# A graph, attention and expert block on one core: expert weights merged by TensorE in groups of 32 columns, with four reorderings

## The chip, the core and the metric

One NeuronCore of a Trainium2 chip runs the whole program. The engines are TensorE (PE, with its weight loads as PEld), VectorE (DVE), ScalarE (ACT), GpSimd (POOL) and SyncE (SP), which issues the DMA transfers. The metric is the device time in microseconds.

## The reference

Input x has 1250 rows of 512 numbers, and 41,250 directed edges (src, dst). All is float32. Cut to what matters:

```python
# graph branch: linear + PReLU, then two layers of
agg = segment_sum(x[src], dst); h = prelu((x + agg) @ W1.T + b1) @ W2.T + b2
x = relu(batch_norm(h))
# mix branch (8 heads of 64): softmax(q) per row, softmax(k) over the rows
context = einsum('bnhd,bnhe->bhde', softmax_k, v / N); out = (q / 8) . context
mix = layer_norm(out @ w_out + b_out) * ln_scale
# expert layer on x2
gh = relu(x2 @ gfc1.T + b); g = (gh @ gfc2.T + b).mean(rows)      # 8 numbers
W1m = W1 + sum_e g[e] * tv_W1[e]; W2m = W2 + sum_e g[e] * tv_W2[e]  # 8 experts
b1m, b2m likewise; h = relu(x2 @ W1m.T + b1m); out = h @ W2m.T + b2m
result = (a layer norm of x2 + out) with merged scale and shift, added to the block's input
```

The expert weights of one kind are 8 matrices of 512 x 256 numbers, 8.4 MB for both kinds, and g is the same for all rows.

## The kernel before

The 1250 rows are 10 tiles of 125 (T), or 5 chunks of 250 columns when transposed (J). The 512 features are 4 blocks of 128 (KB). Every product is done in float16 with a high and a low part: 3 matmuls per block of the contraction, so 12 for a tile of 125 x 512 ("natural tile", `natural_tile`, L543 to L560) or for a block of 128 x 250 (`product`); all of them are issued by the line L462 of `passes`. ScalarE writes the high half of a result, VectorE the low half. GpSimd writes the low halves of the weights (`split_weight`, L1753).

Each engine has its own program, written out by hand in order; semaphores connect them. PSUM has 8 banks, given out in families: USES lists the phases of a family in order, RING its number of banks, and BANKS_FROM names what of another family must be read before a phase may take its banks. `wait_bank` turns this into waits.

Stages that the change touches:

**Query and value products (QV), from 120 us.** TensorE does the first 7 query tiles, then value and query tiles by turns, then value tiles alone. After each value tile comes a window: VectorE makes one-hot matrices of 15 edge columns (L1173 to L1185), its offsets (L1180) go to TensorE, which loads 15 addresses, multiplies the one-hots into a count bank (L448, L451), and ScalarE copies the counts to the adjacency matrix (L808). For each query tile VectorE takes maxima (L1359), subtracts (L1360), sums the exponentials (L1364), and GpSimd multiplies the tile by the reciprocal sums (L1771), in one loop over the ten tiles, when the sums are there.

**Mix, from 190 us.** The contexts times w_out give the m products in banks 0 to 3 (family z). Query tiles are flipped (`flip_q`, 4 transposes, L543) into two x banks; the loop over t flips tile t+4, then multiplies mix tile t into bank t % 2 (family n), then does a window. VectorE's loop does the window, the low part of tile t+4 (`low_tile_t`), then reads the mix tile (L1414). The first aggregation (agg0, L650) follows, in banks 0 to 3; it also needs the diagonal that VectorE adds (L1401).

**Expert layer, from 397 us.** Two 4 MB transfers bring tv, the expert weights (L420, L421), once the last down product is done. After the gate products (to 440.9 us) one small float32 matmul sums g. ScalarE makes 4 diagonal matrices g[e] * identity (L1106). TensorE multiplies expert matrices with them (`merge_on_pe`, L745), 128 x 512 results in float32, for 4, 3, 4 and 3 of the 8 experts of the four parts (two column halves of W1, two halves of W2: PE_SHARE); VectorE adds the other experts one at a time with scalar_tensor_tensor in halves of 256 (L1622) and then the bank of TensorE (L1629). ScalarE makes the high half of each part (L1110, L1116), VectorE the low half (L1195). TensorE's order: merge W1 part 0, the b2 matmul (L760), merge W1 part 1, ffn1 products 0 to 4, merge W2 parts 0 and 1, ffn1 products 5 to 9, then the ten last products (ffn2, `natural`, a bias matmul L772 and 6 more each) in two banks. `hidden(i)` on ScalarE and `low_hidden(i)` on GpSimd (L1814) turn an ffn1 product into the transposed hidden layer; the b2 row is split on GpSimd after `low_hidden(1)`.

**The tail.** The last tiles are handled in units of one or two tiles (UNITS). For a unit u VectorE adds the residual with row sums (L1682), scales the sums (L1686, row_minus), does `finish_unit(u - 1)` (reciprocal L1699, the add to the output for tiles that aren't GpSimd's, L1704) and `centre(u)` (L1692). ScalarE squares (L1138), takes the root (L1143) and then scales GpSimd's tiles of the unit before (`scale_unit`, L1132); GpSimd adds x for the tiles 1, 3, 5 and 7 (L1835). SyncE stores the tiles in order (L425), two transfers a tile.

Of the kernel before, what the change touches and what calls it, by code (L numbers as in the profile page):

```python
# [20 lines left out]
F32 = mybir.dt.float32  # L21
# [8 lines left out]
P = 125  # L30
# [46 lines left out]
PE_EXPERTS = 4  # L77
PE_SHARE = (4, 3, 4, 3)
# [8 lines left out]
for _t in range(T):  # L87
# [17 lines left out]
BANKS_FROM = {"qv": ("t", "k", 17), "mix": ("z", "m", 1), "agg0": ("n", "mix", 9), "ffn2": ("t", "ffn1", 9),  # L105
              "up1": ("x", "qt", T - 1), "rows": ("u", "up1", T - 1), "gnn": ("u", "up1", T - 3)}
# [18 lines left out]
UNITS = [(0, 1), (2, 3), (4, 5), (6, 7), (8,), (9,)]  # L125
# [28 lines left out]
def gps_block(nc, dram):  # L154

    with ExitStack() as ctx:
# [33 lines left out]
        def tr16(r, blocks=KB):  # L190
# [34 lines left out]
        g_diag = ohs[:, 2 * KB * CH + 6 * D:2 * KB * CH + 6 * D + PE_EXPERTS * 256].bitcast(F32).rearrange(  # L225
            "p (e n) -> p e n", e=PE_EXPERTS)
# [119 lines left out]
        def wait_bank(pe, family, phase, i, slot):  # L346
# [9 lines left out]
            if phase in BANKS_FROM:  # L356
                source, last, uses = BANKS_FROM[phase]
                if slot < min(RING[family], RING[source]):
                    wait_done(pe, source, last, uses + slot)
# [26 lines left out]
        def _(sp):  # L386
# [43 lines left out]
        def _(pe):  # L430
# [198 lines left out]
            for t in range(T):  # L629
                if t + 4 < T:  # L630
                    flip_q(t + 4)
# [109 lines left out]
            def merge_on_pe(bank_, part, share):  # L741

                for k in range(PE_EXPERTS - share, PE_EXPERTS):
                    pe.wait_ge(diag_ready, k + 1)
                    last = nc.tensor.matmul(bank_, g_diag[:, k, :], part(E - PE_EXPERTS + k), start=(k == PE_EXPERTS - share),  # L745
                                            stop=(k == PE_EXPERTS - 1))
                last.then_inc(pe_merged, 1)

            def merge_w1(bank_, m):
                merge_on_pe(ps[:, bank_, :].rearrange("p (k f) -> p k f", k=KB),  # L750
                            lambda e: tv[:, 0, e, :].rearrange("p (k f) -> p k f", k=KB)[:, :, m * 128:(m + 1) * 128], PE_SHARE[m])

            def merge_w2(bank_, h):
                merge_on_pe(ps[:, bank_, :], lambda e: tv[:, 1, e, h * D:(h + 1) * D], PE_SHARE[FB + h])

            pe.wait_ge(got_tv, 32)
# [1136 lines left out]
```

## Time and profile before

| | |
|---|---|
| median of 3 runs | 502.27 us (501.51 to 503.23) |
| the profiled execution | 499.22 us, its span 497.4 us |
| PE busy | 459.6 us, 92% |
| PEld / DVE / ACT / POOL busy | 357.8 / 324.2 / 250.1 / 168.9 us |
| chain of waits | PE 76%, DVE 13%, ACT 5%, issue 3%, POOL 2% |
| mean granted clock of TensorE | 0.989 |

The span is what the profiler saw from the first to the last instruction; the execution's own time holds 1.8 us around it. "Busy" of PE includes time in which a matmul waits in the pipe. The chain of waits is followed back from the last instruction, each step to what released it; "issue" is time for which the profile shows no cause. L with a number is a line of the kernel; where a helper issues everything, the tile names tell instructions apart.

### The profile page before, as it was taken

Reading aid. Unit: us, or ns where it says so; the run is one execution under the profiler, and the core shown is the slowest. Engines: PE = TensorE matmul, PEld = TensorE weight load, DVE = VectorE, ACT = ScalarE, POOL = GpSimd, SP = SyncE. Lnnn points to the kernel's source line nnn. Section 1 sums busy time; section 2 is a strip of 40 time slices with the busy share of each in tenths; the row PEclk is TensorE's granted clock in tenths of the full one; section 3 lists DMA queues with packets and bytes.
Section 4 is the critical chain, followed back from the end, with each engine's and each line's share of the span. In section 5 each row is a group of like instructions: output and inputs, shape, how many; then the busy total and the mean of one; then the engine's idle time right before and its main releaser. Section 6 shows DMA issues by size and latency. Waiting matters only on the chain.

```text
span 497.4 us, 9899 instructions
## 1 busy us (share of the span) xinstructions
PE 459.6 (92%) x3564; PEld 357.8 (72%) x3564; DVE 324.2 (65%) x749; ACT 250.1 (50%) x527; POOL 168.9 (34%) x176
## 2 busy tenths in 40 slices
PE   2999999999999998999999999999999969989892
PEld 1777668886765676766999995679998858956651
DVE  4777797747999857754655449635333676439787
ACT  4789345147712345244434756424446378734454
POOL 1379453021095003033336990004232124405412
PEclk9999999999999899999999999999999989999998
DMA  8702002202020002011100001000000296000024
GB/s 247 214 3 84 1 0 87 86 1 84 2 86 0 2 3 86 0 40 57 78 0 0 1 2 62 1 0 1 0 3 4 84 402 275 1 0 2 1 60 146
DMA packets 5246, 27.44 MB, mean 55 GB/s; under 512 B 1036, under 2 KB 1161, under 8 KB 3544
## 3 DMA queue, kind: packets, MB, share of 16 engines
q1 hardware_dynamic: 5208, 26.92, 15.6%
q8 instruction: 25, 0.41, 0.4%
q14 instruction: 13, 0.11, 0.1%
HBM read 24.36 MB, written 2.56 MB: 54 GB/s over the span
## 4 chain that ended last, share of the span: by engine, by line
PE 76%; DVE 13%; ACT 5%; issue 3%; POOL 2%; DMA 1%; SPq 0%; DVEq 0%; ACTq 0%
PE ps L462 47%; PE ps L650 17%; PE ps L451 4%; PE ps L745 3%; POOL late L1745 2%; PE ps L543 2%; PE ps L553 1%; DVE r L1692 1%; DVE late L1195 1%; DVE r L1704 1%; PE ps L448 1%; ACT r L825 1%; DVE ohs L1185 1%; DVE r L1682 1%; DVE offsets L1180 1%
## 5 line engine op out<-in xcount | busy, mean ns | idle before, releaser
L462 PE MATMUL ps<-r,wslot 128*128 128x250 f16 x840 | 95.3, 272 | 3.5 <-DVE r L1194 3.3
L462 PEld LDWEIGHTS ps<-r,wslot 128*128 128x128 f16 x840 | 81.5, 98 | 14.9 <-DVE r L1194 5.2
L650 PE MATMUL ps<-late,r 125*128 (+1 forms) x800 | 87.1, 269 | 1.0 <-DVE r L1414 1.0
L650 PEld LDWEIGHTS ps<-late,r 125*128 125x128 f16 x800 | 77.5, 97 | 10.9 <-issue 1.7
L1753 POOL TENSOR_TENSOR wslot<-stage,wslot 128x512 f16<-128x512 f32 x32 | 39.5, 1265 | 133.3 <-ACT wslot L797 133.3
L462 PE MATMUL ps<-wslot,r 128*125 128x512 f16 x300 | 70.5, 386 | 0.0
L462 PEld LDWEIGHTS ps<-wslot,r 128*125 128x125 f16 (+1 forms) x300 | 40.9, 139 | 22.1 <-issue 1.4
L1781 POOL TENSOR_TENSOR late<-ohs,late 128x250 f16<-128x250 f32 x40 | 25.7, 652 | 86.9 <-ACT late L980 86.9
L462 PE MATMUL ps<-late,wslot 128*128 (+1 forms) x480 | 51.7, 269 | 0.0
L462 PEld LDWEIGHTS ps<-late,wslot 128*128 128x128 f16 x480 | 46.5, 97 | 5.4 <-issue 0.8
L808 ACT ACTIVATE late<-ps 125x500 f16<-125x500 f32 x25 | 14.7, 588 | 68.6 <-PE ps L451 68.6
L462 PE MATMUL ps<-wslot,late 128*125 128x512 f16 x216 | 48.9, 380 | 0.2 <-DVE late L1486 0.2
L1467 DVE TENSOR_SCALAR ohs<-ohs,cols 128x250 f32<-128x250 f32 x40 | 16.7, 419 | 42.4 <-ACT ohs L975 42.4
L462 PEld LDWEIGHTS ps<-wslot,late 128*125 128x125 f16 x216 | 28.8, 136 | 15.9 <-issue 0.6
L975 ACT ACTIVATE ohs<-ps,bias_a 128x250 f32<-128x250 f32 x40 | 18.6, 467 | 31.4 <-PE ps L650 29.2
L1195 DVE SCALAR_TENSOR_TENSOR r<-ps,r 125x512 f16<-125x512 f32 (+1 forms) x30 | 20.2, 683 | 20.4 <-ACT r L821 13.5
L1175 DVE TENSOR_TENSOR ohs<-iota,sources 125x1920 f16<-125x1920 f16 x25 | 29.8, 1192 | 0.1
L451 PEld LDWEIGHTS ps<-ohs 125*128 125x128 f16 x375 | 22.5, 97 | 8.3 <-issue 0.2
L821 ACT ACTIVATE r<-ps 125x512 f16<-125x512 f32 x20 | 11.9, 596 | 32.6 <-PE ps L462 32.1
L1027 ACT ACTIVATE r<-ps,cols 128x250 f32<-128x250 f32 x40 | 18.2, 465 | 20.0 <-PE ps L462 20.0
L462 PE MATMUL ps<-late,r 128*125 128x512 f16 x120 | 27.3, 380 | 0.0
L451 PE MATMUL ps<-ohs 125*128 125x70 f16 x375 | 26.4, 197 | 0.0
(186 smaller groups left out, 734.7 us busy)
## 6 DMA issues: line engine op xcount, KB each, us to landing
late<-in_tv SPq DMA_DIRECT2D x2, 4096.0 KB, 18.1
x<-in_x SPq DMA_DIRECT2D x5, 448.0 KB
out<-r SPq DMA_DIRECT2D x10, 224.0 KB
stage<-in_w_up SPq DMA_DIRECT2D x2, 1024.0 KB, 5.3
stage<-in_w_down SPq DMA_DIRECT2D x2, 1024.0 KB, 5.5
stage<-in_w_lin SPq DMA_DIRECT2D x1, 1024.0 KB, 6.0
stage<-in_w_k SPq DMA_DIRECT2D x1, 1024.0 KB, 4.8
stage<-in_w_q SPq DMA_DIRECT2D x1, 1024.0 KB, 5.0
```

The costliest lines, as they stand in the source:

```text
L451: mm_ = nc.tensor.matmul(ps[:, 6 + slot, bass.ds(at[c], SPAN)], oh_s[:, slot, c, :], oh_d[:, slot, c, :], start=False, stop=(c == WC - 1))
L462: last = nc.tensor.matmul(out, stat_(hs, b), mov(hm, b), start=start and n == 0, stop=stop and n == 3 * blocks - 1)
L650: last = nc.tensor.matmul(bank("t", m), u_nat[layer][:, p, h, m * 128:(m + 1) * 128], counts(h)[:, chunk], start=(start and h == 0 and p = ...
L745: last = nc.tensor.matmul(bank_, g_diag[:, k, :], part(E - PE_EXPERTS + k), start=(k == PE_EXPERTS - share), stop=(k == PE_EXPERTS - 1))
L808: nc.scalar.activation(adj[:, :, w * WIN:(w + 1) * WIN], ps[0:P, 6 + w % 2, 0:WK].rearrange("p (d h) -> p h d", h=T), ACT.Copy, accum_out= ...
L975: nc.scalar.activation(act_tmp[:, m, :], bank("t", m), ACT.Identity, bias=bias_a[:, KB * layer + m:KB * layer + m + 1], scale=S_H / S_X).t ...
L1027: nc.scalar.activation(gnn_t[:, m, j * CH:(j + 1) * CH], bank("t", i % KB), ACT.Identity, bias=col("b2", KB * layer + m), scale=1 / (S_W * ...
L1175: nc.vector.tensor_tensor(oh_s[:, slot].rearrange("p c (s r) -> p c s r", r=RUN), iota_s.unsqueeze(1).to_broadcast([P, WC, 128 // RUN, RUN ...
L1195: return nc.vector.scalar_tensor_tensor(out, src, scale, hi, ALU.mult, ALU.subtract)
L1467: nc.vector.tensor_scalar(negative[:, q, :], act_tmp[:, q, :], 0.0, col("conv_a", layer), ALU.min, ALU.mult).then_inc(neg_ready, 1)
L1753: last = nc.gpsimd.tensor_tensor(wslot[:, i % SLOTS, 1, k, :], stage[:, k * D:(k + 1) * D], wslot[:, i % SLOTS, 0, k, :], ALU.subtract)
L1781: nc.gpsimd.tensor_tensor(a_t[:, 1, m, chunk], act_tmp[:, m, :], a_t[:, 0, m, chunk], ALU.subtract).then_inc(tmp_free, 1)
```

## The change

- **Merges.** PE_EXPERTS and PE_SHARE go. The 128 rows of an expert block are 4 groups of 32. tv is loaded so that partition group e % 4 holds expert e, and the four groups of its rows lie beside each other (slots 4 * (e // 4) + j). One matmul then contracts over 4 experts x 32 rows and gives 32 output rows: stationary is a stack of 4 scaled identities (32 columns), moving are 512 columns, output is a quarter of a bank's partitions. Two sets of 4 experts, 4 groups, 4 parts: 32 matmuls. VectorE's and ScalarE's merging work is gone but for one add per part; VectorE makes the stacks. The b2 matmul and both W2 merges stand after ffn1 product 4; W1 part 1 uses bank 4 and W2 part 0 bank 5.
- **Loads.** 16 transfers of 512 KB instead of 2 of 4 MB.
- **ScalarE's and GpSimd's order.** High half of W1 part 1 before the hidden chunks, both high halves of W2 after chunk 4; b2's split after `low_hidden(4)`.
- **Queries.** GpSimd multiplies query tiles 7 to 9 after the 20th window's one-hots.
- **Mix.** The flip of tile t+4 stands behind mix tile t on TensorE, its low part behind the mix read on VectorE; family n takes banks 2 and 3.
- **Tail.** Units (0), (1,2), (3,4), (5,6), (7,8), (9) instead of (0,1), (2,3), (4,5), (6,7), (8), (9); the row sums are scaled on ScalarE.

```diff
-PE_EXPERTS = 4
-PE_SHARE = (4, 3, 4, 3)
+GROUP = 32
+GROUPS = 128 // GROUP
+SETS = E // GROUPS
-BANKS_FROM = {"qv": ("t", "k", 17), "mix": ("z", "m", 1), "agg0": ("n", "mix", 9), "ffn2": ("t", "ffn1", 9),
-              "up1": ("x", "qt", T - 1), "rows": ("u", "up1", T - 1), "gnn": ("u", "up1", T - 3)}
+BANKS_FROM = {"qv": ("t", "k", (17, 18, 19, 20)), "mix": ("z", "m", (3, 4)), "agg0": ("n", "mix", (0, 0, T - 1, T)),
+              "ffn2": ("t", "ffn1", (7, 8)), "up1": ("x", "qt", (T - 1, T, 0, 0)), "rows": ("u", "up1", (T - 1, T)),
+              "gnn": ("u", "up1", (T - 3, T - 2))}
-UNITS = [(0, 1), (2, 3), (4, 5), (6, 7), (8,), (9,)]
+UNITS = [(0,), (1, 2), (3, 4), (5, 6), (7, 8), (9,)]
-            return ps[:, {"z": 0, "n": 0, "x": 4, "y": 6, "u": 4}[family] + slot, :]
+            return ps[:, {"z": 0, "n": 2, "x": 4, "y": 6, "u": 4}[family] + slot, :]
...
+            grouped = dram["tv"].rearrange("(j i) w e n -> i w j e n", j=GROUPS)
             for w in range(2):
-                sp.dma_start(tv[:, w], dram["tv"][:, w]).then_inc(got_tv, 16)
+                for e in range(E):
+                    own, at = slice(e % GROUPS * GROUP, (e % GROUPS + 1) * GROUP), e // GROUPS * GROUPS
+                    sp.dma_start(tv[own, w, at:at + GROUPS, :], grouped[:, w, :, e, :]).then_inc(got_tv, 16)
...
             for t in range(T):
-                if t + 4 < T:
-                    flip_q(t + 4)
                 wait_done(pe, "x", "qt", t + 1)
...
                 natural_tile("n", "mix", q_t, mm, t, t)
+                if t + 4 < T:
+                    flip_q(t + 4)
...
+            def merge_on_pe(bank_, part):
+
+                for set_ in range(SETS):
+                    pe.wait_ge(diag_ready, set_ + 1)
+                    for j in range(GROUPS):
+                        last = nc.tensor.matmul(bank_[j * GROUP:(j + 1) * GROUP], g_stack[:, set_, :], part(GROUPS * set_ + j),
+                                                start=(set_ == 0), stop=(set_ == SETS - 1))
                 last.then_inc(pe_merged, 1)
...
             merge_w1(6, 0)
-            pe.wait_ge(g_vec, 1)
-            nc.tensor.matmul(ps[0:P, 7, :], grow[:, :], tvrow[:, 2, :], start=True, stop=True).then_inc(b2_sum, 1)
-            merge_w1(5, 1)
+            merge_w1(4, 1)
             for m in range(FB):
                 pe.wait_ge(wm_split, m + 1)
                 for j in range(J):
                     product("ffn1", J * m + j, (J * m + j) % 4, w1m, m, x2_t, slice(j * CH, (j + 1) * CH))
                 if m == 0:
-                    merge_w2(4, 0)
+                    pe.wait_ge(g_vec, 1)
+                    nc.tensor.matmul(ps[0:P, 7, :], grow[:, :], tvrow[:, 2, :], start=True, stop=True).then_inc(b2_sum, 1)
+                    merge_w2(5, 0)
                     merge_w2(6, 1)
...
             high_w1(0)
             act.wait_ge(b1_done, 1)
+            high_w1(1)
             for i in range(FB * J):
                 hidden(i)
-                if i == 1:
-                    high_w1(1)
-                if i in (J - 1, 2 * J - 2):
-                    high_w2(int(i > J))
+                if i == J - 1:
+                    high_w2(0)
+                    high_w2(1)
...
             for u, tiles in enumerate(UNITS):
+                wait_done(act, "n", "ffn2", tiles[-1] + 1)
+                part = slice(tiles[0], tiles[-1] + 1)
+                nc.scalar.activation(row_minus[:, part], row_sum[:, part], ACT.Copy, scale=-1 / D).then_inc(minus_ready, 1)
                 act.wait_ge(minus_ready, u + 1)
...
-                if t + 4 < T:
-                    low_tile_t("qt", q_t, t + 4, S_Q)
                 wait_full(dve, "n", "mix", t)
                 nc.vector.scalar_tensor_tensor(mix_nat[:, t, :], bank("n", t % 2)[0:P, :],
                                                1 / (S_Q * S_M * DH ** 0.5 * N), rows[:, 0, :], ALU.mult, ALU.add
                                                ).then_inc(free["n", "dve"], 1)
+                if t + 4 < T:
+                    low_tile_t("qt", q_t, t + 4, S_Q)
...
+            for set_ in range(SETS):
+                last = nc.vector.scalar_tensor_tensor(g_picked[:, set_, :], gcol[:, GROUPS * set_:GROUPS * (set_ + 1)], 1.0,
+                                                      in_group[:, :], ALU.mult, ALU.mult, accum_out=g_own[:, set_:set_ + 1])
+            then(last)
+            for set_ in range(SETS):
+                nc.vector.tensor_scalar(g_stack[:, set_, :], of_group[:, :], g_own[:, set_:set_ + 1], None, ALU.mult
+                                        ).then_inc(diag_ready, 1)
...
-                wait_done(dve, "n", "ffn2", UNITS[u][-1] + 1)
-                part = slice(UNITS[u][0], UNITS[u][-1] + 1)
-                nc.vector.tensor_scalar(row_minus[:, part], row_sum[:, part], -1 / D, None, ALU.mult).then_inc(minus_ready, 1)
...
+            soft_q(0, Q_FIRST)
+            pool.wait_ge(oh_ready, first_window("mix"))
+            soft_q(Q_FIRST, T)
...
-            for i in range(2):
+            for i in range(J):
                 low_hidden(i)
             pool.wait_ge(b2_added, 1)
```

## Rows read from the trace of the kernel before

**Rows 1.** Chain of waits, 443 to 471 us: start, length, engine, tile, line, count.

```profile
443.40 3.67 PE ps L745 x8
447.07 1.05 PE ps L760 x2
450.89 6.40 PE ps L462 x60
457.30 6.01 PE ps L745 x14
469.92 0.70 DVE wslot L1195
471.05 0.40 PE ps L772
```

**Rows 2.** Chain of waits, 151 to 170 us.

```profile
151.89 1.44 DVE ohs L1185
...
157.18 1.02 DVE offsets L1180
158.20 1.19 issue
159.39 0.37 PE ps L448
...
161.50 4.39 PE ps L462 x12
165.89 0.21 PE ps L448
...
169.22 0.21 PE ps L448
```

**Rows 3.** Timeline, 156 to 167 us: start, length, engine, line, operation, operands.

```profile
156.29 1.88 POOL L1771 TENSOR_TENSOR r<-r,qsum  x1 [3.53 <-DVE qsum L1365]
...
165.94 0.15 DVE L1180 TENSOR_SCALAR offsets<-base 1x16 int32<-1x16 f32 x1
...
166.35 0.71 DVE L1185 TENSOR_TENSOR ohs<-iota,rel 125x1050 f16<-125x1050 f16 x1
```

**Rows 4.** Two us of the stretches: busy of PE, PEld, DVE, ACT, POOL; granted clock, DMA.

```profile
162.00:164.00 2.00, 2.00 (x6) 1.09 (x5) 1.62 (x3) 0.70 (x3) 0.67 (x1) 0.50 0.03 8
```

**Rows 5.** Chain of waits, 194 to 231 us.

```profile
194.99 0.60 DVE r L1195
...
195.72 0.62 PE ps L543 x4
...
230.07 0.61 DVE r L1414
...
230.93 9.14 PE ps L650 x84
```

**Rows 6.** Groups by form, 440 to 497 us: busy us, mean ns, idle before.

```profile
L745 PE MATMUL ps<-late,ohs 128*128 128x512 f32 x28 | 12.7, 599 | 0.5 <-ACT ohs L1106 0.5
...
L1835 POOL TENSOR_TENSOR r<-r,x 125x512 f32<-125x512 f32 x4 | 5.1, 1284 | 15.7 <-ACT r L1132 15.7
...
L1110 ACT ACTIVATE wslot<-stage 128x512 f16<-128x512 f32 x2 | 1.3, 631 | 3.7 <-DVE stage L1629 3.7
```

**Rows 7.** Stretch after the expert loads, columns as in rows 4; last GB/s.

```profile
420.00:424.00 4.00, 4.00 (x40) 3.73 (x39) 2.27 (x8) 2.82 (x10) 1.55 (x2) 1.00 0.02 4
```

**Rows 8.** Chain of waits in the tail.

```profile
483.01 1.32 DVE r L1692 x2
484.33 1.23 DVE r L1682 x4
...
493.51 0.75 DVE r L1704
```

**Rows 9.** Timeline of VectorE in the tail.

```profile
481.65 0.50 DVE L1686 TENSOR_SCALAR qmax<-qmax 125x2 f32<-125x2 f32 x1
```

**Rows 10.** The store line: duration ns min/median/max, first and last start.

```profile
L425 SPq DMA_DIRECT2D out<-r x20: 317/375/425, 479.1 to 494.6; - x20
```

More of the change, by code:

```diff
@@ L739, in _ @@
             nc.tensor.matmul(bank("x", 1)[0:E, 0:P], g_part[:, :], ones[:, 0:P], start=True, stop=True).then_inc(full["x"], 1)
[L741 to L746, printed above, removed]
+            def merge_on_pe(bank_, part):
[4 more added lines that the diff above has]
+                                                start=(set_ == 0), stop=(set_ == SETS - 1))
                 last.then_inc(pe_merged, 1)
@@ L776, in merged_at @@
         def merged_at(part):
-            return sum(2 * (E - n) + 1 for n in PE_SHARE[:part + 1])
+            return part + 1
         @block.scalar
@@ L1101, in _ @@
                     scaled_chunk(4)
-            act.wait_ge(g_col, 1)
-            for k in range(PE_EXPERTS):
-                e = E - PE_EXPERTS + k
-                nc.scalar.activation(g_diag[:, k, :], ident[:, :], ACT.Copy, scale=gcol[:, e:e + 1]).then_inc(diag_ready, 1)
             def high_w1(part):
@@ L1141, in _ @@
                 act.wait_ge(squared, u + 1)
-                part = slice(tiles[0], tiles[-1] + 1)
                 nc.scalar.activation(std[0:P, part], row_square[:, part], ACT.Sqrt, bias=eps[0:P, 2:3], scale=1 / D
@@ L1600, in _ @@
                     normalizer_of(g + 1)
+            then(nc.vector.tensor_reduce(of_group[:, :], ident[:, :].rearrange("p (e i) -> p i e", e=GROUPS), AX.X, ALU.add))
+            then(nc.vector.tensor_reduce(in_group[:, :], ident[:, :].rearrange("p (e i) -> p e i", e=GROUPS), AX.X, ALU.add))
             wait_done(dve, "t", "gate", 20)
@@ L1609, in _ @@
             dve.wait_ge(g_col, 1)
-            dve.wait_ge(got_wm, 16)
-            dve.wait_ge(got_tv, 32)
-            half_done = [0]
-            def merge(total, task, experts):
-                halves = [(total[:, k:k + n], lambda e, k=k, n=n: task(e)[:, k:k + n])
-                          for n in [total.shape[1] // 2] for k in (0, n)]
-                for e in range(experts):
-                    for h, (out, part) in enumerate(halves):
-                        if e:
-                            dve.wait_ge(merged, half_done[0] + 2 * e + h - 1)
-                        nc.vector.scalar_tensor_tensor(out, part(e), gcol[:, e:e + 1], out, ALU.mult, ALU.add).then_inc(merged, 1)
-                half_done[0] += 2 * experts
-                dve.wait_ge(merged, half_done[0])
+            for set_ in range(SETS):
[5 more added lines that the diff above has]
+                                        ).then_inc(diag_ready, 1)
+            dve.wait_ge(got_wm, 16)
             def add_pe_part(total, bank_, n):
@@ L1657, in _ @@
                                     ).then_inc(b2_added, 1)
-            low_w1(1)
             def half(h):
                 return slice(h * D, (h + 1) * D)
-            def merge_w2(h):
-                merge(wm32[:, 1, half(h)].rearrange("p (k n) -> p k n", k=2),
-                      lambda e: tv[:, 1, e, half(h)].rearrange("p (k n) -> p k n", k=2), E - PE_SHARE[FB + h])
             def low_w2(h):
@@ L1828, in _ @@
             pool.wait_ge(b2_ready, 2)
-            for i in range(2, FB * J):
+            for i in range(J, FB * J):
                 low_hidden(i)
```

41 lines of the change are left out of this document (21 added, 20 removed).

## The prediction

> **What bounds the kernel now.** The page first: TensorE is busy 92% of the span and owns 76% of the chain of waits, so time is won where TensorE waits, or where its own work shrinks. The chain of waits in order of time then shows three places that this diff touches. (a) 151 to 166 us, where query and value products alternate with the count windows of the adjacency matrix: the chain leaves TensorE for VectorE and comes back through a TensorE stretch that takes 4.39 us for 12 matmuls [rows 2], though the beat afterwards is 3.33 us for 12 matmuls and a window. (b) The mix stage, 195 to 231 us: the first flip and the first aggregation product each wait for a VectorE read [rows 5]. (c) 443 to 471 us: the expert merges on TensorE (14 float32 matmuls, 28 passes), the two halves of the first expert layer between them, and a gap before the last products [rows 1]. From there VectorE's beat per pair of tiles sets the end [rows 8, 9]. Between 231 and 440 us nothing changes.
>
> **Query tiles later, part (a).** VectorE's window writes its offsets in 0.15 us and its second one-hot in 0.71 us when GpSimd is idle, but in 1.02 and 1.44 us beside GpSimd's query multiply, which itself takes 1.88 us [rows 2, 3]. The change moves the last three of ten multiplies behind the last value window. That takes away 0.7 us of the one-hot at 151.89 and 0.87 us of the offsets at 157.18: VectorE is 1.6 us earlier. TensorE then loads its 15 addresses (the 1.19 us of issue at 158.20) beside running matmuls instead of idle. The idle was followed by the granted clock 0.50 [rows 4], the lower of the two levels, 1.2 GHz, and by 4.39 us where 2.62 would do (the beat of 3.33 less a window of 0.71). Sum: the window at 165.89 moves up. Going forward from 154.5 without the overlaps I get TensorE's next windows at about 157.9 and 161.6, against 159.39 and 165.89: 4.2 us, of which at least 1.8 hangs on the clock staying up. Bounds: zero (VectorE's next wait takes it all) to 5.0 (all of the excess from 154.04, where two beats of 3.33 would do for 11.7). I take 4.2, since everything after 165.89 runs on TensorE's own beat and hands it on. The moved multiplies run from some 176 us, with no window left on VectorE, and are first needed by a flip after 200 us; GpSimd's next work, a weight split, waits for ScalarE until 187 us. That is free.
>
> **Mix stage, part (b).** The first mix tile needs only the last of the four m products read (194.99), not the flip before it that waits until 195.72 for a bank: 0.7 us of idle goes; the flip's own work stays. With the mix products in banks 2 and 3, aggregation blocks 0 and 1 (banks 0, 1) need no mix read any more, only the diagonal, done at 230.07; before, both waited for the last read at 230.07 plus 0.61, and began at 230.93. That is 0.85 us. Blocks 2 and 3 ask for reads that are over by then. VectorE reads the mix tile before the low part of tile t+4, which has two or three beats to spare. Part (b): -1.55 us, between 0 and -2.5 (nearest row: the 1.5 us that the two gaps are).
>
> **Gate tiles.** Two small reductions are added while VectorE waits for the gate; nothing waits for them. After the gate vector, four ScalarE diagonals (first one out 0.4 us later) are replaced by two VectorE products with a sum and two scalings, 0.17 to 0.25 us each, the first stack out some 0.65 us later. +0.25 us.
>
> **Expert merges, part (c).** Before: 14 matmuls of 512 columns, float32, two passes each, 0.43 us a pass (6.01 us for 14 passes), 12.0 us in all; VectorE merges the other 18 experts. After: 4 parts x 2 sets x 4 groups = 32 matmuls, each with 32 stationary columns, thus 64 passes of the same 512 moving columns. No matmul in the trace has neighbours that write other partitions at the same time, so the price is bounded from both sides: one after the other 64 x 0.427 = 27.3 us; four at a time 6.8 us. I take a middle that follows from what the rows show of order. Every float32 matmul comes as two passes in sequence [rows 6]; both passes of a group write the same partitions, so the second must follow the first; passes are taken in program order, so the next group's first pass can go only beside the second pass of this one. Then a matmul costs one pass time instead of two: two parts in a row, 16 matmuls, take 16 pass times and one to drain, 17 x 0.427 = 7.26 us. The Trainium skill, TensorE: Matmul & The Clock Gate (Part 3: Packing small matmuls), gives 2.38 times for three column groups and says that matmuls start and end strictly in program order; no run here shows either yet. By its first figure alone the merges would lie near the lower bound, by its second they lie where I put them.
>
> The path with 7.26: merges start 443.40 + 0.25 = 443.65; the first part is out at 447.4, its add (taken as long as the low half, 0.70), its high half (0.63 [rows 6]) and its low half (0.70 [rows 1]) end at 449.6 with hand-overs, covered; both W1 parts end 450.9 and the first layer's first half starts at 451.0 (before 450.89 on the chain, 450.73 by its first matmul). It takes 6.4: 457.4. The b2 matmul moves here, 1.05: 458.45. W2: 7.26, against 6.01 before: 465.7. Second half 6.56: 472.3. Before, the last product then waited 1.35 us for the ScalarE high and VectorE low half of W2 (469.92 to 471.05), as VectorE's merge of the last experts had come late. Now both halves of W2 are added as soon as their bank is done and are split during the second half (hidden chunk 5 stands behind both high halves on ScalarE, which end 1.4 us after the merge; its product ends 1.3 us after it), so the last products start at 472.35 instead of 471.05: +1.3 us, gate included. The b2 vector is summed at 458.4; its four GpSimd steps, and the low hidden chunks queued behind them, have until 472. Banks 2 and 3 of the last products ask for hidden chunks 7 and 8, done before.
>
> **The tail.** Per pair VectorE pays two residuals 1.23, the row-sum scaling 0.42 with its wait (the instruction took 0.50 us [rows 9]), a reciprocal, one add 0.75, two centrings 1.32: 3.92 us [rows 8]. The scaling goes to ScalarE (0.3 us, behind the same read, beside VectorE's reciprocal and add), leaving 3.5 per pair, still above TensorE's 3.0. Played forward, tile 9's residual ends 18.75 us after the start of the last products (before 20.6). But the units change: tile 7 is now with tile 8. Its ScalarE scaling stands behind tile 9's squares and root, so it ends at 21.05, GpSimd's add (1.28 [rows 6]) at 22.4, and the store queue goes in order of tiles: stores of 7, 8, 9 are six issues of 0.375 us [rows 10] behind it, against two behind VectorE's end at 23.2 before (494.26 less 471.05). 22.4 + 2.3 = 24.7 against 23.2 + 0.8 = 24.0: +0.7 us. Bounds -1.9 (only the saved scalings count) and +1.5.
>
> **Stores of the expert weights.** 2 transfers of 4 MB become 16 of 512 KB in 4 KB runs. They are issued near 398; the two before were over by 420 [rows 7], and the first merge needs them at 443.6: the rate may halve. 16 issues at 0.375 us are 6 us on SyncE's queue, which has nothing behind them until the first store at 479.
>
> **Sum** against the profiled execution (499.22 us; span 497.4): -4.2 - 1.55 + 1.3 + 0.7 = -3.75. That execution is 3.0 us under the median of the runs; I carry the difference over: 502.27 - 3.75 = 498.5 us. A change of 0.3%, 1.5 us, is about what a measurement of this kernel can tell from none.
>
> **Rivals.** (1) Four groups at once. Merges fall to 3.4 us per pair of parts. Part W1a is out at 445.4, its add and halves take 2.1 with hand-overs, first half at 447.55; +6.4, +1.05, +3.4, +6.6: last products at 465.05, 6.0 earlier than before. Sum -4.2 - 1.55 - 6.0 + 0.7 = -11.05: 491.2 us. For it: passes on different output partitions share nothing that a row shows. Against it: the paired passes. (2) The other side: the groups do not overlap. Two parts of W1 are 32 passes, 13.7 us against 7.3 with b2 before; W2 13.7 and b2 1.05 against 6.0; less the gap of 1.3: last products 14 us later. Sum +8.95: 511.2 us, slower. For it: all 28 passes here stand end to end, and each would stream its 512 columns in full. The merges decide from 17.6 us on: below an overlap of 1.55 the change loses. (3) Part (a) gives nothing because TensorE falls to 1.2 GHz anyway or VectorE waits elsewhere: with the forecast's merges 502.3, no change. (4) The expert weights land late. The Trainium skill, DMA: Bandwidth & Descriptors (table of pitfalls), has 164 GB/s for rows 2 MiB apart in memory, which is the distance of the four runs of a partition here; an estimate by it has them landed at 398 + 51 = 449 us. Worked from the rows: 22 us before, at 0.4 of that rate 55, landed at 453 instead of needed at 443.6, and all behind it moves by 9.4: 507.9 us. Against it: the loads of x, 4 KB rows too, move 247 GB/s in the first slice of the page, and 8.4 MB at that rate are 34 us, in time.
>
> **How the numbers follow.** Forecast 0.42, (1) 0.30, (2) 0.18, (3) 0.07, (4) 0.03. Faster by over 0.3%: the forecast and (1) less the forecast's upper edge, 0.68. Within: that edge and (3), 0.11. Slower: (2) and (4), 0.21. The likeliest's own range is 495.5 to 501; the range reaches down over (1), 489.5, and up to 508, leaving out (2).
>
> **What would show it.** Right: starts of neighbouring merge passes 0.2 us apart on average; first half near 451; no clock below 1.00 between 158 and 166; merges (all four parts) 14 to 15 us; tile 7's GpSimd add as the last work but the stores. Wrong: merges of 7 or 27 us; a window still 1.0 us in its offsets; the first merge waiting for a transfer.

## The result, and the profile after

The changed kernel takes 493.97 us (median of 4 runs, 492.1 to 497.75) against 502.51 us before (4 runs, 501.51 to 503.23): ratio 0.9841, 95% interval 0.9807 to 0.9874, thus 6.3 to 9.7 us faster. Its profiled execution took 494.36 us, span 491.9. One execution among all that follow, of the kernel rest_alone at 504.24 us, was in a slower state of the chip and is left out of every figure. The page after: span and busy times, TensorE's clock and the DMA rate in 40 slices, the chain by engine.

```profile
span 491.9 us, 9954 instructions
PE 455.7 (93%) x3600; PEld 356.5 (72%) x3600; DVE 306.5 (62%) x715; ACT 250.2 (51%) x529; POOL 164.7 (33%) x176
PEclk9999999999999999999999999999999969998997
GB/s 249 218 3 79 8 0 88 87 1 85 1 88 0 2 3 85 1 69 44 63 0 0 1 2 62 1 0 1 0 1 5 85 190 214 213 69 1 3 53 156
PE 82%; DVE 9%; ACT 3%; POOL 2%; issue 2%; DMA 1%; SPq 0%; DVEq 0%; ACTq 0%
```

VectorE has 18 us less to do and TensorE owns more of the chain. The expert layer is where most of the time went. Chain of waits after, 430 to 464 us, against [rows 1]:

```profile
430.98 7.70 PE ps L473 x72
...
441.38 5.32 PE ps L757 x32
446.70 6.52 PE ps L473 x60
453.22 1.05 PE ps L778 x2
454.27 3.57 PE ps L757 x32
457.84 6.51 PE ps L473 x60
464.35 0.22 PE ps L784
```

L757 is the merge, L473 the products, L778 the b2 matmul, L784 the bias of the last products. Both W2 parts, 32 passes of 512 columns, take 3.57 us. One pass takes 0.427 us here, so 8 times four passes are 3.42: the four groups run at once. Two short stretches at the start of W2, merge passes of TensorE alone (stretch, its length, busy time and number of passes that touch it, granted clock, DMA):

```profile
454.20:454.25 0.05, 0.05 (x4) 1.00 0.00 0
454.25:454.65 0.40, 0.40 (x4) 1.00 0.00 0
```

Four passes begin in the first 0.05 us and no fifth in the next 0.40. So they are not cheap passes one after another. The W1 parts, the same 32 passes, take 5.32. Two-microsecond stretches of the two merges, columns as in [rows 4]:

```profile
442.00:444.00 2.00, 2.00 (x13) 0.54 (x8) 0.00 (x0) 0.00 (x0) 0.00 (x0) 0.51 0.00 0
454.00:456.00 2.00, 2.00 (x21) 0.60 (x24) 0.68 (x1) 0.09 (x1) 1.51 (x3) 1.00 0.00 0
```

The granted clock is 0.51 in the first (the lower level, 1.2 GHz) and 1.00 in the second: W1 pays half speed for most of its merge.

The value and query stage, chain after, 154 to 179 us, against [rows 2]:

```profile
157.95 0.15 issue
158.10 0.37 PE ps L459
158.47 1.74 PE ps L462 x15
160.21 2.70 PE ps L473 x12
162.91 0.21 PE ps L459
...
178.40 0.37 PE ps L459
```

The 1.19 us of issue is 0.15, and the 12 matmuls of 4.39 us take 2.70. The mix stage, against [rows 5]:

```profile
192.52 2.80 PE ps L473 x12
195.33 0.43 PE ps L554 x4
...
224.17 2.00 DVE late L1411 x10
226.17 1.22 issue
227.40 12.66 PE ps L661 x117
```

The first mix tile follows VectorE's read with no flip ahead of it; the first aggregation product comes 1.22 us after the diagonal, not at once. The groups of the end (434 to 492 us) and its timeline, against [rows 6, 8]:

```profile
L757 PE MATMUL ps<-late,ohs 128*32 128x512 f32 x64 | 9.0, 712 | 0.6 <-DVE ohs L1627 0.6
L1696 DVE SCALAR_TENSOR_TENSOR r<-r,rstd,x 125x512 f32<-125x512 f32 x6 | 6.7, 1115 | 0.2
L1833 POOL TENSOR_TENSOR r<-r,x 125x512 f32<-125x512 f32 x4 | 5.3, 1328 | 15.4 <-ACT r L1140 15.4
```

```profile
483.08 1.26 POOL L1833 TENSOR_TENSOR r<-r,x 125x512 f32<-125x512 f32 x1 [2.56 <-ACT r L1140]
483.18 1.71 DVE L1696 SCALAR_TENSOR_TENSOR r<-r,rstd,x 125x512 f32<-125x512 f32 x1
485.16 1.51 POOL L1833 TENSOR_TENSOR r<-r,x 125x512 f32<-125x512 f32 x1 [0.82 <-ACT r L1140]
485.66 1.56 DVE L1696 SCALAR_TENSOR_TENSOR r<-r,rstd,x 125x512 f32<-125x512 f32 x1
486.70 2.46 SPq L436 DMA_DIRECT2D out<-r  x6
```

The last two adds of VectorE took 0.77 and 0.75 us before (the last one is in [rows 8]) and now take 1.71 and 1.56: each lies beside an add of GpSimd. The end hangs on something else. GpSimd's add of tile 7 ends at 486.68, and the six store issues of tiles 7, 8 and 9 follow it without a gap; tile 9's come at 488.35, 1.1 us after VectorE had done with it.

To compare kernels stage by stage, the profiled time of each is cut at five instructions on the path: A, from the last product of the query tiles' steady beat of 3.46 us (129.87 us before, 130.17 after) to the start of the last window of the value tiles; B, on to the first aggregation product; C, on to the end of the gate products; D, on to the start of the last products; E, on to the end of the span. "Clock" is the mean of 180 to 200 us. Where it is 0.91, the lower level, 0.50, was granted for some microseconds of them (181.4 to 184.8 in banks_undone), and the upper for the rest. The same two microseconds in banks_undone and in after:

```profile
182.00:184.00 2.00, 2.00 (x22) 2.00 (x20) 0.00 (x0) 2.00 (x3) 0.73 (x1) 0.50 0.00 0
182.00:184.00 2.00, 2.00 (x40) 2.00 (x38) 0.00 (x0) 1.97 (x2) 0.00 (x0) 1.00 0.03 8
```

```
               ratio [95%]               A      B     C       D      E     clock
before         1                         51.07  49.99 209.99  30.13  26.35  1.00
after          0.9841 [0.9807, 0.9874]   48.23  49.00 211.28  25.51  27.71  1.00
after_again    0.9834 [0.9812, 0.9856]   48.22  49.17 211.16  25.58  27.58  1.00
groups_alone   0.9898 [0.9871, 0.9924]   50.62  52.02 210.98  26.07  26.34  0.91
rest_alone     0.9944 [0.9913, 0.9976]   48.22  48.87 210.33  30.13  27.52  1.00
q_undone       0.9899 [0.9869, 0.9928]   50.64  50.69 211.32  25.48  27.59  0.91
sets_inner     0.9885 [0.9839, 0.9931]   48.23  49.17 211.31  25.80  27.39  1.00
units_undone   0.9821 [0.9781, 0.9861]   48.22  48.82 211.16  25.59  25.81  1.00
pool_three     0.9852 [0.9815, 0.9889]   48.22  48.82 210.35  24.41  27.11  1.00
keep_warm      0.9829 [0.9800, 0.9857]   48.22  50.70 211.12  24.40  27.56  0.91
tv_rows        0.9840 [0.9807, 0.9872]   48.27  48.63 211.36  25.49  27.65  1.00
banks_undone   one run, 496.75 us        48.28  50.47 211.13  25.77  27.66  0.91
flips_undone   one run, 497.37 us        48.23  51.66 210.32  26.04  27.65  0.91
best           0.9788 [0.9759, 0.9817]   48.22  50.45 211.26  24.41  25.84  0.91
```

From before to after: A -2.84, B -0.99, C +1.29, D -4.62, E +1.36, and +0.30 ahead of A: -5.5 us, the difference of the spans.

### The profile page after: what moved, and what is told of

Read it like the earlier page. It is cut to its first block, busy times and chain, and to the rows that moved or that the text cites. A ratio compares the mean times of both kernels' runs of the same rounds, so it can differ in the third digit from the quotient of the medians.

```text
span 491.9 us, 9954 instructions
## 1 busy us (share of the span) xinstructions
PE 455.7 (93%) x3600; PEld 356.5 (72%) x3600; DVE 306.5 (62%) x715; ACT 250.2 (51%) x529; POOL 164.7 (33%) x176
## 4 chain that ended last, share of the span: by engine, by line
PE 82%; DVE 9%; ACT 3%; POOL 2%; issue 2%; DMA 1%; SPq 0%; DVEq 0%; ACTq 0%
PE ps L473 52%; PE ps L661 17%; PE ps L462 4%; PE ps L554 2%; POOL late L1737 2%; PE ps L757 2%; PE ps L564 1%; DVE r L1696 1%; DVE r L1684 1%; PE ps L459 1%; DMA x<-in_x 1%; DVE r L1204 1%; ACT r L843 1%; DVE late L1205 1%; DVE r L1677 1%
## 5 line engine op out<-in xcount | busy, mean ns | idle before, releaser
L473 PE MATMUL ps<-r,wslot 128*128 128x250 f16 x840 | 96.7, 274 | 2.9 <-DVE r L1204 2.7
L473 PEld LDWEIGHTS ps<-r,wslot 128*128 128x128 f16 x840 | 82.1, 99 | 15.2 <-DVE r L1204 4.4
L473 PE MATMUL ps<-wslot,r 128*125 128x512 f16 x300 | 68.8, 380 | 0.0
L473 PEld LDWEIGHTS ps<-wslot,r 128*125 128x125 f16 (+1 forms) x300 | 40.1, 136 | 21.2
L473 PE MATMUL ps<-late,wslot 128*128 (+1 forms) x480 | 51.7, 269 | 0.0
L473 PEld LDWEIGHTS ps<-late,wslot 128*128 128x128 f16 x480 | 46.6, 97 | 5.3 <-issue 0.8
L473 PE MATMUL ps<-wslot,late 128*125 128x512 f16 x216 | 48.9, 380 | 0.2 <-DVE late L1496 0.2
L473 PEld LDWEIGHTS ps<-wslot,late 128*125 128x125 f16 x216 | 28.8, 136 | 15.9 <-issue 0.6
L1185 DVE TENSOR_TENSOR ohs<-iota,sources 125x1920 f16<-125x1920 f16 x25 | 28.8, 1152 | 0.1
L473 PE MATMUL ps<-late,r 128*125 128x512 f16 x120 | 27.4, 381 | 0.9 <-DVE late L1205 0.9
```

Source lines behind the costliest of these rows:

```text
L473: last = nc.tensor.matmul(out, stat_(hs, b), mov(hm, b), start=start and n == 0, stop=stop and n == 3 * blocks - 1)
L1185: nc.vector.tensor_tensor(oh_s[:, slot].rearrange("p c (s r) -> p c s r", r=RUN), iota_s.unsqueeze(1).to_broadcast([P, WC, 128 // RUN, RUN ...
```

## The experiments

The kernels below start from the changed one unless they say otherwise. They were timed in three sets, each on one chip together with the kernel before, which took 502.87, 501.76 and 503.1 us there; ratios compare across the sets, medians do not.

**The two halves of the change, and the change again.** groups_alone keeps the grouped merges with their loads and orders, and takes back the rest:

```diff
-UNITS = [(0,), (1, 2), (3, 4), (5, 6), (7, 8), (9,)]
+UNITS = [(0, 1), (2, 3), (4, 5), (6, 7), (8,), (9,)]
-            return ps[:, {"z": 0, "n": 2, "x": 4, "y": 6, "u": 4}[family] + slot, :]
+            return ps[:, {"z": 0, "n": 0, "x": 4, "y": 6, "u": 4}[family] + slot, :]
...
-            soft_q(0, Q_FIRST)
-            pool.wait_ge(oh_ready, first_window("mix"))
-            soft_q(Q_FIRST, T)
+            with pool.Fori(0, T) as t_:
```

(the flips, their low parts and the row sums too go back to where they were). rest_alone is the opposite: PE_EXPERTS, PE_SHARE, two 4 MB transfers and the old orders come back, all else stays. after_again is the changed kernel, unedited.

> The change without its small parts: query multiplies, flips, banks of the mix and last products, units and the scaling of the row sums are as before; only the merges in groups, their loads, and the order of merges, b2 and high halves stay. Theory (the merges overlap fourfold and carry most of the gain): W2 merges 3.5 us for 32 matmuls, last products about 5 us earlier than before relative to the gate's end, ratio to before 0.990. Rival (the small parts carry it, the merges only swap work): ratio 0.997 to 1.000. Forecast's theory (two passes of a group in sequence): merges 7 us a pair, ratio 1.00.

> The complement: merges, loads and their order as before, all small parts as changed. Theory: the last value window 2.5 us and the first aggregation product 3.5 us earlier than before, tail no shorter, ratio 0.993. If the parts were worth what the forecast said (4.2 + 1.55 - 0.7): ratio 0.990. Rival: they give nothing by the end, because the gate stage waits longer: ratio 1.00.

> The changed kernel once more beside the others. Ratio 0.984 again. If the stretch at 1.2 GHz between 397 and 407 us and at the W1 merges is a matter of the single execution, it differs in this profile; if it belongs to the kernel, it is there again.

groups_alone 497.78 us, rest_alone 499.36, after_again 493.73. The halves give -1.02% and -0.56%, their sum -1.58%; the whole gives -1.66%. The merges are thus the larger half, about 5 us, and the halves add up within the intervals of 0.2 to 0.3 points. In after_again the clock of 0.50 near 400 us and in W1 is there again. D falls only with the groups (26.07 against 30.13 us in rest_alone), A only with the rest (the 0.45 us by which groups_alone is under before is about what the low clock of [rows 4] costs, see q_undone).

**The order of the passes.** sets_inner exchanges the loops, so that four passes in a row write the same 32 partitions:

```diff
-                for set_ in range(SETS):
-                    pe.wait_ge(diag_ready, set_ + 1)
-                    for j in range(GROUPS):
+                pe.wait_ge(diag_ready, SETS)
+                for j in range(GROUPS):
+                    for set_ in range(SETS):
```

> The changed kernel with the two loops of the merge exchanged: both sets of a group one after the other, then the next group, so four passes in a row go to the same 32 columns. If passes start in program order and one that must wait holds back those behind it: 13 passes a part, a W2 pair 25 passes = 10.7 us instead of 3.6, a W1 pair likewise, time +12 us (ratio to before 1.01). If every group of columns has its own queue: a pair stays at 3.6 us, no change (0.984). If only the two passes of one matmul are handled apart: in between.

Chain of waits of sets_inner, its W1 and its W2 merges:

```profile
441.33 5.36 PE ps L757 x32
...
454.36 3.61 PE ps L757 x32
```

The start of its W2, columns as in the same view of after:

```profile
454.28:454.34 0.06, 0.05 (x4) 1.00 0.00 0
454.34:454.73 0.39, 0.39 (x4) 1.00 0.00 0
```

3.61 us against 3.57, and 5.36 against 5.32: the order inside a part hardly matters. Here too four passes begin together, though the first four of the program all write the same 32 partitions. (The ratio, 0.9885, has an interval of 0.9839 to 0.9931 that reaches over that of the change; no stretch of the profile differs by more than 0.3 us.) So passes that wait for others of their own group do not seem to hold back the groups behind them in the program; the records don't name the group of a pass, so that the four that begin together are of four groups is inferred. Either way the explanation of the forecast falls here, and not only its number.

**Query tiles.** q_undone takes back soft_q alone, by the last four lines of the first diff.

> The changed kernel with GpSimd's ten query multiplies in one loop again. Theory: the last value window comes 2.5 us later than in the changed kernel, VectorE's offsets take 1.0 us three times, time +2.5 us (ratio to before 0.989). Forecast: +4.2 us (0.992). Rival: another wait takes its place, +0 to 1 us.

497.81 us, 0.65 points above after_again on the same chip (each ratio is uncertain by 0.2 to 0.3): about 3.3 us. In the profile A grows by 2.42 us. The times may hold more than the queries: in five of the six executions of q_undone TensorE's mean clock was 0.977, in those of after_again 0.980 to 0.987, and its profile has the 0.50 after 180 us. Chain of waits of q_undone, 158 to 167 us:

```profile
158.28 1.02 DVE offsets L1190
159.30 1.19 issue
160.49 0.37 PE ps L459
...
162.59 2.70 PE ps L473 x12
165.51 1.61 PE ps L462 x15
```

The waits of [rows 2] are back, instruction by instruction. But the 12 matmuls after them take 2.70 us, not 4.39: after the same 1.19 us of idle the clock stayed at 1.00 in this execution, and in groups_alone (2.70 too). The low clock of [rows 4] was an event of one execution, and it cost little there. At clock 1.00 TensorE's next window takes 1.61 us (165.51) instead of the 0.50 before, so that from the late window to the second one after it 9.33 us pass in q_undone (160.49 to 169.82), and 9.83 before (159.39 to 169.22).

**The mix stage.** Two kernels, each run once: banks_undone puts the mix products back in banks 0 and 1 and the last products with them, flips_undone puts the flip of tile t+4 ahead of mix tile t again (and its low part ahead of the read):

```diff
# banks_undone
-            return ps[:, {"z": 0, "n": 2, "x": 4, "y": 6, "u": 4}[family] + slot, :]
+            return ps[:, {"z": 0, "n": 0, "x": 4, "y": 6, "u": 4}[family] + slot, :]
# flips_undone
+                if t + 4 < T:
+                    flip_q(t + 4)
                 natural_tile("n", "mix", q_t, mm, t, t)
-                if t + 4 < T:
-                    flip_q(t + 4)
```

> The changed kernel with mix and last products in banks 0 and 1 again. Forecast: first aggregation product 0.85 us later after the diagonal (from 1.2 to some 2.1 us after it). Theory from the trace after, where 1.2 us of issue stand between the diagonal and the product: the product waited for the engine's own jump into the aggregation code, and the banks are worth 0.3 us at most. The last products start 0.1 us or less later.

> The changed kernel with the flip ahead of the mix tile on TensorE and its low part ahead of the mix read on VectorE again. Forecast and theory: the end of the first mix tile comes 0.7 us later after VectorE's last m product than in the changed kernel; the later tiles keep the beat of 3.76 us. Rival: the mix read is what VectorE is late with, and the beat grows.

Both have the clock 0.91 between 180 and 200 us, so B is compared with keep_warm and best (50.70 and 50.45), which share it. flips_undone has 51.66: the flips give 1.0 to 1.2 us, by one execution each. banks_undone has 50.47: the banks give nothing. Its chain, from the diagonal to the first aggregation product:

```profile
226.87 1.99 DVE late L1411 x10
228.86 0.61 DVE r L1422
229.48 0.56 issue
230.04 9.99 PE ps L661 x92
```

With the old banks the product waits for the mix read, 0.61 us, and then 0.56 of issue; with the new ones 1.22 of issue. From the diagonal it is 1.17 us and 1.22. So something of TensorE's own fills this time, hidden behind the read before. In all profiles of the study TensorE rests 0.98 to 1.54 us between the last mix product and the first aggregation product, whatever else is done. A branch on the register that was loaded before the last mix tile stands in the program there; that it is the cause was not tested.

**The low clock in the W1 merge.** keep_warm adds matmuls whose result nobody reads, ahead of the waits for the gate vector and for the first stack:

```diff
+            def filler(n):
+                for _ in range(n):
+                    nc.tensor.matmul(ps[:, 7, :], weight("gate")[:, 0, 0, 0:128], x2_t[:, 0, 0, 0:512], start=True, stop=True)
+
+            wait_done(pe, "y", "gnn", T)
+            filler(6)
...
+            filler(2)
```

> The changed kernel with eight idle matmuls of 128 x 512 (their result is not used) on TensorE: six while it waits for the gate sums, two while it waits for the stacks. Theory (the gap of 2.6 us before the merges brings the clock 0.50 that all profiles with grouped merges show at the W1 merges, 5.3 us for what takes 3.6 us at W2): clock 1.00 in the merges, W1 pair 3.6 us, first half of the first layer 1.1 us earlier relative to the gate's end, ratio 0.982. Rival (the clock falls because of the 32-column matmuls themselves or of what ran before): still 0.50 at the merges, ratio 0.984.

The W1 merge and the product after it, first in after_again, then in keep_warm (its merge is L763):

```profile
440.83 5.33 PE ps L757 x32
...
446.19 6.58 PE ps L473 x60
```

```profile
443.82 1.95 PE ps L763 x16
...
448.00 6.58 PE ps L473 x60
```

In keep_warm the first part takes 1.95 us and the product waits for its split; from the start of the merge 4.18 us pass, against 5.36. D is 24.40 instead of 25.58. So the low clock in W1 costs 1.2 us. Two stretches at this place, of after_again and of rest_alone, whose merges are 128 columns wide:

```profile
442.00:444.00 2.00, 2.00 (x16) 0.75 (x12) 0.02 (x1) 0.00 (x0) 0.00 (x0) 0.50 0.00 0
```

```profile
442.00:444.00 2.00, 2.00 (x6) 0.65 (x4) 1.58 (x5) 0.00 (x0) 0.00 (x0) 1.00 0.00 0
```

TensorE idles twice at the gate ahead of them, 1.39 and 0.60 us in after_again, 1.33 and 0.47 in rest_alone. Nine of the twelve profiles with grouped merges had the low clock there; the other three are the two with the filler (keep_warm, best) and pool_three, which has none, has idles of 1.40 and 0.60 and the same D, 24.41. Both profiles with the wide merges, before and rest_alone, kept the clock. So the low clock is likely behind the new gate, not certain; whether the narrow merges or the 0.2 us more of idle bring it was not tested, and pool_three warns that two executions with the filler don't prove that it always holds the clock up. In the times of keep_warm nothing shows (0.9829 against 0.9834 for the change): 1.2 us are a quarter of a per cent, less than these intervals.

**The loads.** tv_rows stores the expert weights in memory in the order in which the transfers want them, so that each of the 16 transfers reads 16 KB in one run instead of four of 4 KB:

```diff
-                    sp.dma_start(tv[own, w, at:at + GROUPS, :], grouped[:, w, :, e, :]).then_inc(got_tv, 16)
+                    sp.dma_start(tv[own, w, at:at + GROUPS, :], dram["tv"][own, w, at:at + GROUPS, :]).then_inc(got_tv, 16)
```

> The changed kernel with the expert weights laid out in memory as they are wanted in SBUF: the same 16 transfers of 32 partitions, but 16 KB in a row for each partition instead of four runs of 4 KB that lie 2 MB apart. Theory (the runs or their distance halve the rate, 210 against 420 GB/s): the weights land in 20 to 24 us instead of 40; nothing waited for them, so the time stays at a ratio of 0.984 to before. If the long transfer is what stretches the gate stage (44.5 us from the first transfer to the last gate product against 43.3 and 43.7 with the two old transfers): the stage is 0.9 us shorter, ratio 0.982. Rival (32 partitions at a time are what halves the rate): 40 us again.

No change in the time. Four microseconds of the load in tv_rows, and in rest_alone (two transfers of 4 MB):

```profile
428.00:432.00 4.00, 4.00 (x40) 3.69 (x39) 0.86 (x3) 3.48 (x9) 2.50 (x2) 1.00 1.06 225
```

```profile
408.00:412.00 4.00, 3.94 (x36) 3.29 (x35) 3.21 (x7) 3.27 (x10) 2.50 (x2) 1.00 1.06 459
```

The DMA engines are fully busy in both and move half as much with 32 partitions per transfer, in runs of 4 KB (213 GB/s on the page of after) and of 16 KB alike. The run length and the 2 MiB between runs are not what limits them. Whether it is the 32 partitions or the smaller transfers (512 KB against 4 MB) that halve the rate was not tested apart. The load lasts 40 us instead of 22 and is over near 434.5, 7 us before the first merge.

**The tail.** units_undone takes the old units; pool_three leaves tile 7 to VectorE with the new units:

```diff
# units_undone
-UNITS = [(0,), (1, 2), (3, 4), (5, 6), (7, 8), (9,)]
+UNITS = [(0, 1), (2, 3), (4, 5), (6, 7), (8,), (9,)]
# pool_three
-    return t % 2 == 1 and t < T - 2
+    return t % 2 == 1 and t < T - 4
```

> The changed kernel with the units of before, (0,1), (2,3), (4,5), (6,7), (8), (9); row sums still scaled on ScalarE. Theory (tile 7 in the unit before the last makes GpSimd's add and VectorE's two last adds exclude each other, and stores queue behind it): the tail from the first of the last products to the span's end gets 0.5 to 1.5 us shorter than the 27.7 us of the changed kernel, ratio 0.982. Rival (the early start of unit 0 is worth more): longer by 0.5 us, 0.985.

> The changed kernel with tile 7's last add on VectorE instead of ScalarE and GpSimd (tiles 1, 3, 5 stay there). Theory: VectorE pays 0.75 us more but its two adds of 1.71 and 1.56 us go back to 0.75, so its end comes 1.0 us earlier, and stores of 7, 8, 9 no longer wait for GpSimd: time -1.2 us, ratio 0.981. Rival (the long adds are not GpSimd's doing): VectorE's end 0.7 us later, ratio 0.985.

E is 25.81 us in units_undone, 27.58 in after_again: the new units cost 1.8 us. In the times it is hardly seen: the ratio, 0.9821, is 0.0013 or 0.7 us under that of after_again, inside the intervals. The last add of units_undone, with no GpSimd add beside it:

```profile
485.50 0.75 DVE r L1696
```

Moving the row sums to ScalarE with the old units leaves E at 25.81 against 26.34 in groups_alone: 0.5 us gained. In pool_three E is 27.11: taking tile 7 from GpSimd gives back 0.5 of the 1.8. Its last store issues:

```profile
482.17 4.17 SPq L436 DMA_DIRECT2D out<-r  x10
```

GpSimd's add of tile 5 ends at 482.14, and now the ten issues of tiles 5 to 9 stand behind it without a gap. The queue of stores sets the end in both kernels with the new units; in units_undone the last two issues wait for VectorE's last add instead (486.25 and 486.28).

**A version from the findings.** best has the old units, tile 7's add on VectorE, the stored order of tv_rows and the filler: the four diffs above.

> The changed kernel with the units of before, tile 7's last add on VectorE, the weights laid out as in tv_rows and the eight filler matmuls before the merges. Theory: tail 25.3 us instead of 27.5 (units 1.9, GpSimd's add 0.3), W1 merges at clock 1.00 (1.2 us): 3.3 us less than the changed kernel, ratio 0.977. Rival (the clock falls elsewhere instead and the stores set the tail): 0.982.

492.76 us (490.9 to 493.78), ratio 0.9788 [0.9759, 0.9817]. It beats the kernel before for certain, and has the lowest ratio of all; against the change (0.9834 with an upper half-width of 0.0022) it is about 0.5% lower, just where the two intervals touch. In its profile D is 24.41 and E 25.84, as in the kernels that its parts come from; 25.3 had been expected for E.

## Why the prediction was right, and where it was not

The forecast was 498.5 us; 493.97 was measured, inside the range and on the side that was given 0.68. But the case that it was made for, at 0.42, is not what happened. Rival 1 is: four groups at once, 491.2 us. The forecast case had 495.5 to 501 as its own range, which the measured time missed; the whole range held it because it was drawn over rival 1. Step by step:

- **Merges: the step that failed.** "Passes are taken in program order, so the next group's first pass can go only beside the second pass of this one." A pair of parts was put at 7.26 us; W2 took 3.57 (rival 1 said 3.4), and sets_inner, which by that sentence should have been slower still, took 3.61. The Trainium skill, TensorE: Matmul & The Clock Gate (Part 3: Packing small matmuls), says that matmuls start and end in program order; 3.61 us for passes that come in fours to the same group fits no reading of that in which a waiting pass blocks the others. Its 2.38 times for three groups is exceeded here in proportion: 3.8 for four (13.7 us one after the other, over 3.57). The lower bound of the sum, 6.8 us for all 64 passes, was the right end; 8.9 were measured (5.32 + 3.57), 1.2 of them by the clock in W1.
- **What it was worth.** From the gate to the last products +1.3 was forecast, by rival 1 -6.0; D fell by 4.62, and by 5.7 where W1 kept the clock (24.40 in keep_warm). The 1.2 us between are the clock in W1, which neither case had: the trace before showed the low clock after an idle of 1.2 us [rows 2, 4], and the gate leaves one of 1.33 us shortly ahead of W1 (behind which the clock had held before), so the question was there to be asked. The stacks cost what was said: from the end of the gate products to the first merge 2.70 us, against 2.49 before (0.25 forecast).
- **Queries, -4.2.** Right that the waits for VectorE go, size off: A fell by 2.84 against the profile before, and by 2.42 against q_undone, which had no low clock there. The forecast put TensorE's second window at 161.6; it came at 162.6 (162.91 less the 0.3 us that lies ahead of A), because the window at 158.10 still takes 0.37 + 1.74 us, as it did before, where a steady 0.71 was assumed; another 0.45 us is lost in the windows after. And of the 1.8 us that were put down to the clock only 0.5 was in it, by q_undone. Timed, the step is worth 3.3 us, uncertain by 1.9.
- **Mix, -1.55.** B fell by 0.99. The flips gave what was said and a little more (0.7 forecast, 1.1). The banks' 0.85 did not come: behind the read stood 0.56 us and more of TensorE's own. The rows had a hint: the read ended at 230.68 (230.07 + 0.61) and the product began at 230.93 [rows 5], 0.25 us later, where TensorE elsewhere starts 0.04 us after its releaser (192.48 to 192.52 in the profile after).
- **Tail, +0.7.** E rose by 1.36. Direction and cause right (tile 7 late, stores behind it), and its two figures held: GpSimd's add of tile 7 ended 22.5 us after the start of the last products (22.4 forecast), the last store issue at 25.0 (24.7 forecast, 24.0 before). Another 0.3 us lie between that issue and the end of the span (2.70 us against 2.38), by a cause that stays open. No term had the adds of VectorE that coincide with GpSimd's, 1.71 and 1.56 us instead of 0.75: VectorE's end was to come 1.85 us earlier and came 0.2 earlier. It isn't what sets the end of the span here.
- **Weights, rival 4.** Right that the rate would halve, with the right consequence: none. The loads moved 213 GB/s, and tv_rows shows that the distance of the runs isn't what limits them. The Trainium skill, DMA: Bandwidth & Descriptors (Latency and other measured facts), has 164 GB/s where the rows of neighbouring partitions lie 2 MiB apart. The forecast stretched that: here the four runs of one partition lie so, and neighbouring partitions are 64 KB apart.
- **The stretch called unchanged.** C rose by 1.29 us with the clock at 0.50 from 398 to 408 instead of 401 to 404. rest_alone and pool_three, one with the old loads and one with the new, both have only +0.35; so has flips_undone. So neither the loads nor the merges decide it. Why most executions of these kernels have it and the one of before did not stays open.
- **The profile against the median.** The spans differ by 5.5 us, the medians by 8.5. The profiled execution before was 3.3 us under its median, and the forecast carried that over unchanged. TensorE's mean clock goes with it: 0.989 in the profiled one, and 0.978 to 0.987 in each of the 39 executions of before that were timed beside the experiments. So the profile shows before at a clock that none of those had, and the spans understate the change. The clock also splits the times of one kernel: the five executions of rest_alone at 0.988 took 496.3 to 497.7 us, the six at 0.978 to 0.981 took 499.4 to 502.5. The 0.50 after 180 us, in six of the kernels here, is part of it and costs some 1.6 us of B. A difference of two profiles of a few us is safe only stage by stage, with the clocks beside it.
- **Two sums.** By the forecast's own figures the change loses from 18.3 us of merges on (14.5 + 3.75), not from 17.6, and rival 3 is 498.5 + 4.2 = 502.7, not 502.3. Neither moves the forecast or the range.

The errors partly cancel: D was put 5.9 us too dear, queries, mix and tail together 2.6 us too favourable, and C's 1.3 was missing. In the price of the merges the two bounds were 27.3 and 6.8 us; the value in between came from an order of passes that no row showed.

## What to carry to other kernels

Float32 products with few stationary columns can be packed in groups of 32 columns at close to four times the rate, and the order of the groups needs no care; look then at what is bound next and at whether the clock holds in the narrow part. When a wait is removed, read how long the same engine would have needed anyway: a wait that ends 0.2 us before the instruction starts has little to give. Where stores are issued in order, a late tile holds back all behind it, so give the slower engine no tile that is done after its turn. Adds of 125 x 512 numbers on VectorE and GpSimd slow each other when they coincide; count that before moving a tile between units.

## What the runs showed that was not expected

- Four groups of two-pass float32 matmuls overlap in full: 32 passes in 3.57 us, one pass 0.427, in either order; four passes begin within 0.05 us.
- The clock fell to 0.50 in 32-column merges behind the gate in nine of twelve profiles, while 128-column ones at the same place kept 1.00 in both of theirs, behind idles 0.2 us shorter.
- Transfers of 512 KB to 32 partitions moved 205 to 226 GB/s, those of 4 MB to 128 partitions up to 463, with the DMA engines busy in both.
- VectorE's add with two inputs takes 0.75 us alone and 1.56 to 1.72 us beside GpSimd's; both readings of the same instruction come from units_undone and after. In all three such places of after (and in before, 1.30 us at 489.10) it ends 0.54 to 0.55 us after the end of GpSimd's add: 477.72 and 477.18, 484.89 and 484.35, 487.22 and 486.68.
- The same kernel part, at the same instructions, ran at clock 1.00 in some executions and for some microseconds at 0.50 in others (182 to 184 us in after and in banks_undone), at a cost of some 1.6 us.
